# Grouped-query attention with a mixture of experts: another engine copies a round's outputs

## The reference

```python
Q = (x @ Wq + bq).reshape(b, s, 32, 16).transpose(0, 2, 1, 3)
K = (x @ Wk + bk).reshape(b, s, 8, 16).transpose(0, 2, 1, 3)      # repeated for 4 query heads each
V = (x @ Wv + bv).reshape(b, s, 8, 16).transpose(0, 2, 1, 3)
attn = softmax(einsum('bhqd,bhkd->bhqk', Q, K) / sqrt(16))
x = x0 + einsum('bhqk,bhkd->bhqd', attn, V).transpose(0, 2, 1, 3).reshape(b, s, 512) @ Wo + bo
gate_logits = xf @ gate_w.T                                       # xf: layer norm of x
w = softmax(top_k(gate_logits, 2))
out = x + sum over the two chosen experts of w * (xf @ expert_w[e].T + expert_b[e])
```

## Time and profile before

| | us |
|---|---|
| median of 3 runs | 1671.58 |
| lowest, highest | 1670.79, 1673.31 |
| the profiled execution | 1676.17 |
| its span, first to last instruction | 1674.4 |
| mean granted TensorE clock, share of full speed | 0.987 |

### The profile page before, as it was taken

How to read it: one execution, slowest core, us unless ns; L and a number is a source line. 1 busy time by engine, 2 the same in 40 slices (tenths; PEclk the granted TensorE clock), 3 DMA queues, 4 the chain that set the end, 5 groups by cost and what they waited for, 6 DMA issues and landing times.

```text
span 1674.4 us, 36095 instructions
## 1 busy us (share of the span) xinstructions
PE 1619.0 (97%) x13715; PEld 766.8 (46%) x13716; DVE 1439.6 (86%) x1749; ACT 1256.9 (75%) x2352; POOL 575.7 (34%) x858
## 2 busy tenths in 40 slices
PE   6999999999999999999999999999999999978995
PEld 3633444444444444444444444444444444656884
DVE  5488999999999999999999999999999972565565
ACT  3126888888888888888888888888888887204553
POOL 3121243333333333333333333333333344553222
PEclk9999999999999999999999999999999999988998
DMA  7335344423232334233323222323342015585476
GB/s 225 100 107 120 63 110 117 93 69 94 69 88 74 100 76 89 69 94 79 78 69 94 69 71 70 94 69 70 74 106 56 19 48 170 193 276 192 146 269 216
DMA packets 87881, 179.19 MB, mean 107 GB/s; under 512 B 21246, under 2 KB 25342, under 8 KB 86960
## 3 DMA queue, kind: packets, MB, share of 16 engines
q1 hardware_dynamic: 50464, 87.22, 22.3%
q0 software_dynamic: 34624, 88.25, 16.9%
q10 hardware_dynamic: 2640, 1.59, 0.4%
HBM read 91.14 MB, written 86.23 MB: 106 GB/s over the span
## 4 chain that ended last, share of the span: by engine, by line
PE 91%; DVE 2%; DMA 2%; issue 2%; ACT 2%; another core or an unknown queue 1%; SPq 0%; DVEq 0%; POOLq 0%; ACTq 0%
PE bank L1070 35%; PE bank L1033 26%; PE bank L1060 16%; PE bank L1243 6%; PE bank L984 5%; PE bank L1024 1%; PE bank L1272 1%; DMA xs<-slots_x 1%; DMA at_lo<-at_parts 1%; PE bank L1286 1%; DMA y_rows<-ys,tok_i 0%; PE bank L1043 0%; DVE stats L1606 0%; DMA ys<-y_rows 0%
## 5 line engine op out<-in xcount | busy, mean ns | idle before, releaser
L1384 DVE TENSOR_REDUCE max_kc<-bank 128x1 f32<-128x1024 f32 x1024 | 1240.0, 1222 | 49.3 <-PE bank L1033 38.2
L894 ACT ACTIVATE arena_p<-bank 128x512 f32<-128x512 f32 x2048 | 1107.4, 595 | 168.1 <-PE bank L1060 117.1
L1070 PE MATMUL bank<-arena_p,v_cur 128*32 128x256 f32 x8192 | 654.8, 392 | 0.5 <-ACT o_acc L874 0.5
L1033 PE MATMUL bank<-k_st,q_st 48*128 48x512 f32 x2048 | 512.0, 497 | 0.8 <-ACT qf L844 0.8
L1060 PE MATMUL bank<-q_st,k_st 50*128 50x512 f32 x2048 | 432.1, 403 | 0.8 <-ACT arena_p L894 0.8
L1033 PEld LDWEIGHTS bank<-k_st,q_st 48*128 48x128 f32 x2048 | 190.5, 183 | 422.6 <-issue 374.4
L1070 PEld LDWEIGHTS bank<-arena_p,v_cur 128*32 128x32 f32 x8192 | 161.8, 108 | 303.5 <-issue 172.3
L1060 PEld LDWEIGHTS bank<-q_st,k_st 50*128 50x128 f32 x2048 | 268.0, 185 | 37.2 <-ACT arena_p L894 26.2
L537 POOL DMA_DIRECT2D sums<-o_acc x128 | 64.8, 513 | 330.2 <-ACT o_acc L874 325.1
L540 POOL DMA_DIRECT2D sums_rec<-sums x32 | 18.2, 570 | 210.3 <-DVE sums L1414 210.3
L984 PE MATMUL bank<-xT,arena_p 128*128 128x512 f32 x160 | 83.5, 635 | 2.1 <-ACT xT L835 2.1
(11 more groups left out here) (205 smaller groups left out, 1015.8 us busy)
## 6 DMA issues: line engine op xcount, KB each, us to landing
slots_x<-pad_row POOLq DMA_DIRECT2D x27, 1295.0 KB, 6.0
q_st<-q_parts SPq DMA_DIRECT2D x192, 128.0 KB, 4.5
xs<-slots_x SPq DMA_DIRECT2D x39, 259.0 KB
q_parts<-parts SPq DMA_DIRECT2D x16, 512.0 KB, 3.3
we_raw<-in_L_ffn_expert_w POOLq DMA_DIRECT2D x8, 1024.0 KB, 6.0
at_parts<-o_hl POOLq DMA_DIRECT2D x128, 64.0 KB
we_his<-o_hl POOLq DMA_DIRECT2D x32, 256.0 KB, 2.4
we_hi<-we_his SPq DMA_DIRECT2D x8, 1024.0 KB
```

The lines of the kernel that those rows point to most:

```text
L894: act.activation(probs[:, u % PRING, :], bank[:, ring_bank(i, ("score", u)), :], ACT.Exp, scale=SCALE).then_inc(p_ready, 1)
L1033: return pe.matmul(bank[:, 2 + 2 * (m % 2) + q, :], q_st[r:r + CROW, j % SLOTS, h, qt * P:(qt + 1) * P], k_st[r:r + CROW, key_slot(j // NC ...
L1070: mm = pe.matmul(bank[32 * h:32 * h + 32, 6, half], v_cur[:, kt, :], probs[:, (REP * kt + h) % PRING, half], start=(kt == 0 and part == 0) ...
L1384: dve.reduce_max(max_kc[:, m:m + 1], bank[:, 2 + 2 * (m % 2):4 + 2 * (m % 2), :].rearrange("p a s -> p (a s)"), AX.X).then_inc(m_done, 1)
```

## The change

VectorE gets a function copy_outputs of its own, with the same two waits and the same semaphore at its end, and a tensor_copy in place of ScalarE's activation. It calls it in rounds 1 to 30, in step 1 behind the second reduction. ScalarE's copy stays only in round 31, which VectorE has no round_ for, and behind the last round. Nothing else changes: TensorE, GpSimd and SyncE have the same instructions.

```diff
@@ ScalarE, round_
-                    if not first and u == REP * (BEHIND - 1) + 3:
+                    if i == N - 1 and u == REP * (BEHIND - 1) + 3:
                         copy_outputs(i)
@@ VectorE
+            def copy_outputs(i):
+                dve.wait_ge(pv_done, PRING // REP + NKT * i)
+                dve.wait_ge(o_lo, 1 + i)
+                dve.tensor_copy(o_acc[:, :], bank[:, 6, :]).then_inc(o_ready, 1)
@@ VectorE, round_
                         if not isinstance(i, int) or j < N:
                             reduce_unit(j, m + half)
+                        if kt == BEHIND - 1 and half == 1 and not i_is(0):
+                            copy_outputs(i)
                         if kt == 5 and half == 0 and not i_is(0):
                             reciprocal_sums(i)
```

## The result

| | before | changed |
|---|---|---|
| median of 12 runs, us | 1671.01 | 1675.13 |
| lowest, highest, us | 1668.04, 1676.87 | 1672.73, 1679.53 |
| ratio, 95% interval | | 1.0026 [1.0013, 1.0038] |
| the profiled execution, us | 1676.17 | 1676.20 |
| its span, us | 1674.4 | 1674.5 |

By the ratio the change makes the kernel slower by 4.3 us, with an interval from 2.2 to 6.4 us (the two medians are 4.1 us apart), where I forecast 1.5 us faster. It is a small loss, 0.26%, but clear of the noise of these runs. In a later series the same two kernels gave 1.0032 [1.0018, 1.0046].

The account below looks back on a forecast made before the run. TensorE was taken to bound the kernel; relief of ScalarE minus a new wait for VectorE's copy left 0.05 us gained a round, 30 x 0.05 = 1.5 us, from 1671.58 to 1670.1 us. The range was 1665.0 to 1676.0.

Parts of the forecast that it names:

- What bounds the kernel, and the place: TensorE's order, busy 97% of the span; time moves between the first maxima of steps 2 and 3, 2.76 to 2.71 us.
- The copy on VectorE: Behind step 1's second reduction: starts 1.14 us after that reduction's start, lasts 0.69 us, ends at 629.22.
- rival (b): VectorE's copy starts only once the reduction is done, its waits taken then; 0.18 us lost a round, 1677.0 us; chance 0.12.
- (c): The reduction ahead of VectorE's copy drains, copy starts at 628.61; 0.03 us lost a round, 1672.5 us; chance 0.08.
- VectorE's backlog costs nothing: The reductions after the copy run later, but VectorE's 0.41 us idle before step 3's first reduction takes it in.
- The relief of ScalarE: Without its copy, 0.50 us of ScalarE's order, exponential 8 starts at 628.85 and nothing holds scores 11 from 629.45.
- From the copy's end to TensorE's start, 0.06 us: Hand-over from VectorE's copy to values(0) of step 2, sized from reduction 1.1's end to maxima 2.1; values(0) starts at 629.28.
- No row shows values out of a wait: Claimed the profile has no values group starting out of a wait, so its added time was bounded 0 to 0.10 us.
- A group out of a wait is followed 0.05 us later: On TensorE after values(0) of step 2: 0.05 us added to its 0.57 us before scores 10 and 11.
- Scores 10 and 11 take 0.33 us to the next group: On TensorE in step 2: with no wait on an exponential, the pair takes an ordinary pair's 0.33 us, instead of 0.61.
- The bound of the gain, 0.28 us a round: From step 2's to step 3's first maxima, 2.76 us less two ordinary halves of 2.48; 8.4 us at most over 30 rounds.
- The sum: From values(0) at 629.28, terms 0.57, 0.05, 0.33, 0.57 put maxima 3.0 at 630.80 against 630.85: 0.05 us gained a round.

Follow-up runs that it names:

- e4: Kernel before, with an extra VectorE reduction nobody waits for where the change puts the copy, ScalarE keeping its copy; ratio 0.9997 to the kernel before.
- e1: Changed kernel with TensorE's wait for o_ready moved behind its wait for the probabilities; ratio 0.9998 to the kernel before.
- v3: Changed kernel with ScalarE copying 192 columns, then VectorE the rest, TensorE's o_ready wait ahead of that for the probabilities; ratio 1.0011 to the kernel before.
- e2: Kernel before with TensorE's wait for o_ready moved behind its wait for the probabilities; ratio 0.9998 to the kernel before.
- e3: Changed kernel with VectorE's copy cut to 64 of 512 columns; ratio 0.9957 to the kernel before.
- v1: Changed kernel with ScalarE copying 192 columns, then VectorE the rest, TensorE's wait for o_ready last; ratio 0.9972 to the kernel before.
- v2: Changed kernel with ScalarE copying 256 columns, then VectorE 256, TensorE's wait for o_ready last; ratio 0.9983 to the kernel before.

## Why the prediction was wrong

- **What bounds the kernel, and the place:** right. The time moved between maxima 2.0 and 3.0, by 0.19 us a round; 30 x 0.19 = 5.7 us of the 6.2 us by which the attention is longer.
- **The copy on VectorE:** right, start (1.14 us behind the reduction) and length (0.68 against 0.69 us). With it falls rival (b); that its price of 5.4 us came close to the measured 4.3 is an accident, since the copy did start under the tail of the reduction (634.63 against its end at 634.72). With it falls (c) as well, the drain. The prediction held a rule against the trace there and took only half of it: in the Trainium skill's "VectorE: DVE Perf Modes", the section "The DRAIN you can't avoid" adds that a next operation that isn't held starts earlier. The trace agrees with that sentence, by 0.09 us.
- **VectorE's backlog costs nothing:** right, by e4.
- **The relief of ScalarE:** right. Exponential 8 was forecast 0.76 us behind maxima 2.0 and starts there (634.95 against 634.19), and scores 10 and 11 start side by side.
- **From the copy's end to TensorE's start, 0.06 us:** the step that failed, with 0.17 us. I took the price from maxima 2.1, a group with one wait, carried by its weight load. Ahead of values(0) stand two semaphore instructions, and the one that blocks is the first. In that order the load starts 0.23 us behind the signal (in 29 of 30 rounds; once 0.32), with the blocking wait last 0.11 to 0.12. e1, v3 and round 31 show it.
- **"No row shows values out of a wait":** false. The trace of the kernel before has this very wait once, in round 31: the copy ends at 1395.03 and the load starts at 1395.25, as shown above with e2. The summary of who waited for whom had it too, of the kernel before:

```profile
PE bank L1070 <- ACT o_acc L874: 0.5, 1, 0.5
```

Had I followed it, the load of values(0) would have started at 629.22 + 0.22 = 629.44.
- **A group out of a wait is followed 0.05 us later:** wrong too, and on the other side. Values(0) takes 0.57 us to the next group out of the wait (635.57 to 636.14), as without one; what a start out of a wait adds is 0.03 us between its load and its first matmul.
- **Scores 10 and 11 take 0.33 us to the next group:** wrong by 0.10 us. That is their length behind maxima. In step 2 they stand behind values and take 0.43 us, by e3 without any wait. What differs in the trace is that in the ordinary place their weights load 0.23 us ahead of their matmuls, while the maxima run, and behind values load and matmuls start together; that this is the cause was not tested. Round 31 of the kernel before, where scores stand behind values throughout, has it too:

```profile
1397.05 0.50 PE L1060 MATMUL bank<-q_st,k_st 50*128 50x512 f32 x2
1397.48 0.64 PE L1070 MATMUL bank<-arena_p,v_cur 128*32 128x256 f32 x8
```

- **The bound of the gain, 0.28 us a round:** too high for the same reason. I subtracted two ordinary halves, 2.48 us, from 2.76; in the order of step 2 the floor is 2.58, and 0.18 us was to be had.
- **The sum:** with the measured terms, 0.26 us from the copy's end to the first matmul, 0.57 and 0.43, the same chain gives 629.22 + 0.26 + 0.57 + 0.43 + 0.57 = 631.05 for maxima 3.0, 0.20 us late, 6.0 us in all; the trace has 0.19 to 0.20. The mechanism was put down rightly, a wait in place of one taken away. Its two terms of 0.06 and 0.33 us were mis-sized, both by a row from a neighbour that isn't in the same position, and they turned the sign.
- **The range:** 1665.0 to 1676.0 reached 5.9 us above the forecast and holds the median of the changed kernel, 1675.13. That is owed to its width. The direction was wrong, and slower by more than 0.2% had a chance of 0.14.

## What to carry to other kernels

A wait that was free before costs more than the lateness of its signal once it blocks: look for one execution of the same group out of the same wait, which a trace often has in its first or last round, and take the price from there. Put the wait that comes last in time as the last one ahead of the work; here that is worth 0.11 us each time it blocks. And take a group's length from a place with the same neighbours on both sides; a copy that is moved to an engine with room for it can still end later than it did where it was: here 1.12 us behind maxima 2.0, against 0.73.

## What the hardware showed that I had not expected

The waits ahead of one group on TensorE are taken in series, and those that the weight load doesn't carry are instructions of their own, 51 ns long, that start 0.11 us apart when one follows the other. From a signal to the weight load it is 0.05 to 0.06 us when the load carries the wait itself (maxima 2.1), 0.11 to 0.12 us when the wait is an instruction of its own and the last (e1, v1, v2), and 0.22 to 0.23 us when one more such instruction, with a wait long satisfied, stands behind it. The last two hold for signals of ScalarE and of VectorE alike. On TensorE a pair of score matmuls takes 0.33 us to the values that follow when it stands behind maxima and 0.43 us when it stands behind values, with the same instructions and the full granted clock (1.00) in both.
